# Flamingo layer: on VectorE, both sums of probabilities of a group ahead of the low parts of the heads

## What is computed

```python
x = x + tanh(g_xattn[0]) * xattn(ctx_768, layernorm(x), mask, ...)
x = x + tanh(g_ffn[0]) * ffn(layernorm(x), w_router, w1, b1, w2, b2)

# xattn: latents = the 4 x 1024 tokens of 256, context 64 rows of 192, 4 heads of 64
kv = concatenate([layernorm(ctx) @ Wkv.T, ln @ Wlkv.T]); q = ln @ Wq.T
attn = softmax(rmsnorm(q) * SCALE @ rmsnorm(k).T, masked); out = (attn @ v) @ Wo.T + bo
# ffn: softmax router over 8 experts, the two largest per token,
#      gelu(x @ w1[e] + b1[e]) @ w2[e] + b2[e], weighted and summed
```

## Time and profile before

| | |
|---|---|
| median of 3 runs | 915.87 us (913.01 to 918.45) |
| profiled execution | 907.13 us, span 905.4 us, PE clock 0.994 |
| attention with its groups | about 39 to 467 us of the span |
| experts | about 467 to 905 us |
| PE busy, 155 to 212 us (window 2) | 55.12 of 57 us |
| PE busy, 212 to 270 us (window 3) | 53.16 of 58 us |

### The profile page before, as it was taken

How to read it: one execution, slowest core, us unless ns; L and a number is a source line. 1 busy time by engine, 2 the same in 40 slices (tenths; PEclk the granted TensorE clock), 3 DMA queues, 4 the chain that set the end, 5 groups by cost and what they waited for, 6 DMA issues and landing times.

```text
span 905.4 us, 19559 instructions
## 1 busy us (share of the span) xinstructions
PE 850.8 (94%) x5968; PEld 653.0 (72%) x5968; DVE 647.7 (72%) x1500; ACT 513.3 (57%) x1371; POOL 333.6 (37%) x241
## 2 busy tenths in 40 slices
PE   3898999998999989999999999899999999999995
PEld 3654455544455544555459999899999999999995
DVE  5766777668776667677798778866755775576694
ACT  2668876687766977568752754343533443343462
POOL 2332323332286222763144328532332323222233
PEclk9999999999999999999999999999999999999998
DMA  4801000120012201120034549352432535262282
GB/s 128 247 1 50 1 1 1 47 96 1 1 54 88 94 1 47 48 94 12 1 110 120 140 100 275 72 143 47 124 62 47 133 79 109 45 145 47 35 230 27
DMA packets 71895, 70.26 MB, mean 78 GB/s; under 512 B 18592, under 2 KB 66976, under 8 KB 71840
## 3 DMA queue, kind: packets, MB, share of 16 engines
q1 hardware_dynamic: 57696, 52.73, 19.3%
q0 software_dynamic: 13152, 16.86, 10.8%
q10 hardware_dynamic: 992, 0.00, 0.1%
HBM read 44.04 MB, written 26.31 MB: 78 GB/s over the span
## 4 chain that ended last, share of the span: by engine, by line
PE 58%; issue 12%; DVE 10%; POOL 10%; ACT 5%; DMA 3%; SPq 1%; DVEq 0%; POOLq 0%; ACTq 0%
PE psS L1696 18%; PE psF L1892 9%; PE psO L1892 9%; PE psO L1829 6%; PE psS L1813 5%; POOL rr L680 5%; PE psF L1696 4%; POOL routed L690 4%; DVE p_sum L1140 2%; DMA lnf<-routed 2%; PE psF L1860 2%; ACT sq L827 1%; PE psO L1841 1%; PE psO L1696 1%; DMA xr<-in_x 1%
## 5 line engine op out<-in xcount | busy, mean ns | idle before, releaser
L888 ACT ACTIVATE V<-psS,b_col 128x256 f32<-128x256 f32 x280 | 117.1, 471 | 210.1 <-PE psS L1696 191.7
L698 POOL DMA_INDIRECT out<-V,token_i x70 | 124.4, 1777 | 255.7 <-DVE V L1331 234.5
L680 POOL TENSOR_TENSOR rr<-ssm,minus_half 128x4 f32<-128x4 f32 (+1 forms) x72 | 117.2, 1628 | 247.1 <-DVE ssm L1104 247.0
L871 ACT ACTIVATE p_ring<-psS,shift 128x1024 f32<-128x1024 f32 x128 | 136.6, 1112 | 72.3 <-PE psS L1813 71.6
L1829 PE MATMUL psO<-p_ring,V 128*64 128x512 f32 x576 | 148.3, 612 | 0.0
L1140 DVE TENSOR_TENSOR p_sum<-p_sum,p_ring 128x1024 f32<-128x1024 f32 (+1 forms) x112 | 135.9, 1213 | 0.9
L1892 PE MATMUL psF<-ln_hi,K 128*128 128x256 f32 x560 | 123.4, 284 | 0.5 <-DVE K L1310 0.5
L1813 PE MATMUL psS<-Q,K 64*128 64x512 f32 x864 | 120.0, 409 | 0.6 <-ACT p_ring L871 0.5
L1892 PE MATMUL psO<-ln_hi,K 128*128 128x256 f32 x560 | 120.4, 278 | 0.0
L1813 PEld LDWEIGHTS psS<-Q,K 64*128 64x128 f32 x864 | 75.6, 184 | 62.0 <-issue 42.7
L1310 DVE TENSOR_TENSOR K<-V,K 128x512 fp32r<-128x512 f32 x140 | 97.2, 694 | 4.8
(11 more groups left out here) (297 smaller groups left out, 1760.9 us busy)
## 6 DMA issues: line engine op xcount, KB each, us to landing
xr<-in_L_ffn_w SPq DMA_DIRECT2D x11, 1024.0 KB, 4.9
xn<-in_L_ffn_w SPq DMA_DIRECT2D x11, 1024.0 KB, 5.8
lnf<-routed SPq DMA_DIRECT2D x35, 258.0 KB, 2.9
routed<-pad_rows SPq DMA_DIRECT2D x17, 258.0 KB, 9.6
xr<-in_x SPq DMA_DIRECT2D x8, 512.0 KB, 4.5
xb<-in_x SPq DMA_DIRECT2D x4, 1024.0 KB, 5.9
out<-xb SPq DMA_DIRECT2D x4, 1024.0 KB, 4.7
b_raw<-in_L_ffn_b SPq DMA_DIRECT2D x11, 128.0 KB, 6.9
```

What stands on the lines that cost most here:

```text
L680: pool.tensor_tensor(rr[0:p, c % 2, n], ssm[0:p, c % 2, n], minus_half[0:p, n], ALU.pow).then_inc(rr_ready, 1)
L698: pool.indirect_dma_start(out_rows, bass.IndirectOffsetOnAxis(ap=token_i[:, m:m + 1], axis=0), y_out[:, m, :], None, bounds_check=NTOK - 1 ...
L871: act.activation(p_ring[0:p, u % RING, :], psS[u % 2][0:p].rearrange("p a n -> p (a n)"), ACT.Exp, bias=bias).then_inc(exp_done, 1)
L888: act.activation(g32[:, q % 2, (c % 2) * TM:(c % 2 + 1) * TM], psH[q][:, (c % 2) * TM:(c % 2 + 1) * TM], ACT.Gelu_apprx_tanh, bias=b1_col[ ...
```

## The change

On VectorE `add_probabilities(2 * g - 1)` moves from behind `mean_squares` to the place right behind `add_probabilities(2 * g - 2)`, in all groups (before only in group 63). Four smaller edits come with it. The transposes of `Wo` move from group 6 to group 2, to bank 7, and ACT's read of them from group 6 to group 3. The extras `norm` of `i` 2 and 3 move from bank 7 to bank `g % 2`. Both halves of `residual_base` of odd windows stand at `i == 0`, before at 0 and 5. The low part of the first half of `w2` is cut behind the last group, before at `i == 5` of the last window, and that of the second half two activations later.

```diff
@@ mid_uses
-                if w == 0 and i == 6:
+                if w == 0 and i == 2:
                     return [("wo",)]
@@ bank_uses
-                        yield 7 if name[0] in ("out", "norm") and 2 <= i <= 4 else g % 2, name
+                        apart = name[0] == "wo" or name[0] == "out" and i >= 2 or name[0] == "norm" and i == 4
+                        yield 7 if apart else g % 2, name
@@ ScalarE
-                    if g == 6:
+                    if g == 3:
                         output_weights()
@@ VectorE
-                    ahead = w + 1 == WINDOWS and i == 0
-                    if ahead:
+                    if g >= 1:
                         add_probabilities(2 * g - 1)
                     if turned_at(g) is not None:
                         heads_lo(turned_at(g))
                     if tile_at(g) is not None:
                         mean_squares(tile_at(g))
                     if not even and past and not last and i == 3:
                         router_logits(b - 1)
-                    if g >= 1 and not ahead:
-                        add_probabilities(2 * g - 1)
...
-                    if more and not even and i in (0, 5):
-                        residual_base(b, i // 5)
+                    if more and not even and i == 0:
+                        for half in range(2):
+                            residual_base(b, half)
...
-                    if w + 1 == WINDOWS and i == 5:
-                        cut(w2_parts[0:1], 0, w2_ready)
...
-                cut(w2_parts[1:2], 1, w2_ready)
                 dve.wait_ge(w_cut, 1)
-
+                cut(w2_parts[0:1], 0, w2_ready)
                 activate(0, 0)
                 activate(0, 1)
+                cut(w2_parts[1:2], 1, w2_ready)
                 activate(0, 2)
```

## The result

| | before | changed |
|---|---|---|
| first comparison, 12 executions each | 914.49 us (909.28 to 918.45) | 917.72 us (916.08 to 921.79) |
| profiled execution | 907.13 us, span 905.4 | 917.18 us, span 915.4 |

The ratio is 1.004, with an interval of 1.0024 to 1.0057. The changed kernel is slower by 0.4 to 0.6%, some 4 to 5 us by the two ratios, about the 0.5% that the prediction took as the least that can be told; both intervals lie above 1. The time of 917.7 lies beside the forecast of 917.0, but this is partly luck: the sum of the forecast was +1.1 us, and the groups alone got 6.9 us longer.

A forecast was written before the change was run, and what follows sets the result against it. TensorE, busy 94%, bounds the kernel; VectorE counts only where TensorE waits. Terms -4.8 + 9.3 - 0.8 - 1.0 - 0.6 - 1.0 = +1.1 us, on 907.13 about 908, with the 8.7 offset 917 us; range 908 to 926.

The forecast's parts named there:

- The power: On GpSimd, between `ssm` and `qkd`: about 1.0 us instead of 1.91 without a sum beside it; `ssm` to `qkd` 1.27.
- The turns: TensorE's turns of heads waiting for `qkd` in the groups: 5.7 us gained, 0.9 lost, net gain 4.8.
- low parts and `ssm` stand behind one sum more, 1.14: VectorE's loop from `qkd` to `qkd`, with extras x: 4.13 + x becomes 4.35 + x where VectorE sets it, loss 0.22.
- The bank waits: Extra uses of bank `g % 2` on TensorE wait for the later low parts: 9.3 us lost, 0.8 won.
- its own mark: The forecast falls if power stays 1.9, bank waits sum under 5 or over 14 us, or the experts' time changes.
- Groups 29, 30, 47, 48: `norm` moved out of bank 7: 29 loses 0.65 us, 47 loses 0.33, 30 and 48 win 0.4 each.
- `Wo` and the sums of 32 and 50: `Wo` leaving group 6 wins 1.1 us, costs 0.1 in group 2; probability sums of 32 and 50 win 0.5 each.
- the ranks: In groups 33 and 51 `residual_base` leaves, making room for the second sum ahead of the ranks: 0.3 us won each.
- the offset: Profiled execution of the kernel before, 907.13 us, lies 8.7 under the median 915.87; taken over unchanged.
- the balance: Whole kernel: gains at turns and losses at banks offset, time the same, nearly all in 911 to 923; chance 0.60.
- the bank waits come whole: Rival at the banks: each of twelve waits 1.14 or more, some covered ones uncovered; +4 to +9 us, chance 0.13.
- covered groups: Groups 19, 26, 27, 37, 44, 45, 62: ScalarE keeps the low parts anyway, cost zero; uncovered, up to 1.14 us each.

The follow-up runs named there:

- the spare sum: The changed kernel plus an unused two-input sum on VectorE between `ssm` and `qkd` in most groups; 941.43 us, 1.0365 to the kernel before.
- the spare reduction: The changed kernel plus an unused one-input `tensor_reduce` on VectorE between `ssm` and `qkd`; 917.80 us, 1.0098 to the kernel before.
- the order alone: The kernel before with the second sum between low parts and mean squares, without the four smaller edits; 912.84 us, 0.9992 to the kernel before.

## Why the prediction was right, and where its sum was wrong

**The power: right.** 1.0 us in every group (0.7 for the half tiles), `ssm` to `qkd` 1.28 for 1.27. That the sum beside it is the cause was argued from groups 32 and 63; the spare sum, which brings the 1.91 back, shows it.

**The turns: too much by 1.6.** Forecast -4.8. At the turns named the timelines give -4.88 of gains for 5.7, and +1.69 for the four turns with long extras (9, 18, 36, 54) for 0.9, so -3.2. The step at fault: "low parts and `ssm` stand behind one sum more, 1.14", two sums in one piece taken as 2.28. They take 2.46. The program makes the second sum wait for the end of the first, and it starts 0.10 us behind it; apart, with the low parts between, what follows a sum starts before its end, and each costs 1.13 to 1.14. The loop is 4.53 + x and not 4.35 + x, and the four turns with long extras come 0.42 to 0.43 later each, for 0.22. The earlier trace rows already had it, 430.71 - 428.24 = 2.47, and I read those rows only for `ssm` to `qkd`.

**The bank waits: mis-sized, by 5.** The mechanism was right to the group. For groups 9, 11, 12, 18, 25, 28, 36, 43, 54 and 61 the forecast was 8.4 us; the turns behind them come 13.45 later in sum. Of the excess 3.1 is the clock in groups 12 and 28 (1.55 + 1.53 above), which the prediction did not have at all: it priced a wait of TensorE at its length or less. Of the other 2.0, 0.6 is group 61, 1.34 for 0.72, and 1.35 lies in groups 11, 18, 25, 36, 43 and 54, 0.12 to 0.35 each; the 0.18 of two sums in one piece is of that size, but no run takes it apart there. By its own mark, "if the bank waits sum to under 5 or over 14 us", this step of the forecast fell: `norm`, `out` and `turn` wait 17.4 us for `K`, not about 9. The mark itself mixed two things, the length of the waits and what they cost: it named 2.8 us for group 12, which the sum has at 1.17, and `out` and `norm` had waited 2.7 us already before. Single waits were read rightly, 2.81 and 1.28 in groups 12 and 18 for 2.8 and 1.2.

**Groups 29, 30, 47, 48: small as a sum, wrong one by one.** 0.65 and 0.33 of loss and 0.8 of gain were forecast, +0.2 us of loss in all. The turns behind 29 and 47 come 0.6 earlier, those behind 30 and 48 0.3 later, -0.6 in all.

**`Wo` and the sums of 32 and 50: right; the ranks: not.** From the turn of group 3 to that of group 7 it is 1.72 us less (forecast 1.8). The turns of 33 and 51, behind the sums, come 0.70 and 0.71 earlier, for 0.5 each. Those of 34 and 52, behind the ranks, come 0.37 and 0.36 earlier, where 0.3 each for the ranks and 0.61 each for the turn were forecast; the ranks wait 2.3 us for `K` in all, before 1.8. So 1.4 of the 1.6 for both terms was won, but at the sums alone. The experts take 467.8 us behind the turn of group 65, before 465.9, and 466.8 against 466.2 in the second pair of profiles: no change that can be told.

**The sum.** +1.1 was forecast for the groups and +6.9 measured: 1.6 from the turns, 5.1 from the banks, 0.9 won in small ones. The time was hit because the offset was off the other way: 8.7 us between profile and median, of which the 12 executions leave 7.4, and in the profile of the changed kernel 0.5. The kernel before measures 914.49, 913.62, 908.32 and 907.91 us in four series, so a good part of such an offset may be the chip; where the first profile was taken is not known, and this stays open. The second profile of the kernel before, 908.43, lies 0.5 above its median of 907.91. In the ratio the change is 0.4 to 0.6% where 0.1% was forecast: the case was the balance shifted towards the rival "the bank waits come whole", of which the extra waits came but not the uncovering of covered groups. Turns 3 to 65 say 6.9 and the first ratio 3.7 (2.2 to 5.2); the second, 5.2 (3.6 to 6.8), all but reaches it. In the other comparisons of the table medians and turns differ by 2.1 us at most. The gap of the first isn't explained.

## What to carry to other kernels

A move of work on a shared in-order engine has two ends: ask what it stands beside no longer, and what it now stands ahead of. Here, with the edits in place, the first is worth 5.1 us over the turns (-0.54 to -5.63) and the second costs 12.5 (-5.63 to +6.90); a place two instructions further on kept the one without the other. The best kernel of the study is the changed one with one call moved behind `heads_lo`, 0.7 to 0.9% faster than before. Price two instructions of which the second waits for the first from a row that has them in a row. And price a long wait of a busy TensorE (1.9 to 2.8 us here) not at its length alone but with a chance of a slower clock behind it.

## What the runs showed of the hardware

**The granted clock behind a wait.** Behind the wait of 2.81 us in group 12 of the changed kernel (111.56) and that of 1.91 in group 28 (213.73), TensorE's rows read:

```profile
109.00:112.00 3.00, 0.44 (x4) 0.99 0.00 0
112.00:114.00 2.00, 2.00 (x7) 0.50 0.00 0
114.00:117.00 3.00, 3.00 (x19) 0.78 0.00 0
117.00:120.00 3.00, 3.00 (x15) 1.00 0.00 0
...
216.00:219.00 3.00, 3.00 (x28) 0.71 0.00 0
219.00:222.00 3.00, 3.00 (x19) 1.00 0.01 3
```

The wait itself still shows 0.99; the clock falls to 0.50, 1.2 of 2.4 GHz, when the engine works again, and the rows from 117.00 and from 219.00 on show 1.00. It cost 1.5 us both times, and the second profile of the changed kernel has both falls again. The length of the wait alone does not decide. In the kernel with the sum moved and no edits two waits of 2.29 us stand ahead of the same instruction, in groups 33 and 51:

```profile
243.95 0.23 PE L1778 MATMUL psF<-chosen,tri 128*128 128x72 bf16 x1 [2.29 <-DVE K L1125]
361.12 0.21 PE L1778 MATMUL psF<-chosen,tri 128*128 128x72 bf16 x1 [2.29 <-DVE K L1125]
```

with these stretches around them:

```profile
242.00:244.00 2.00, 0.05 (x2) 1.00 0.00 0
244.00:246.00 2.00, 2.00 (x17) 0.50 0.00 0
246.00:248.00 2.00, 2.00 (x13) 0.65 0.00 0
...
359.00:361.00 2.00, 0.00 (x0) 1.00 0.00 0
361.00:363.00 2.00, 1.88 (x21) 1.00 0.00 0
363.00:365.00 2.00, 1.97 (x12) 1.00 0.00 0
```

The first is followed by half the clock, the second by the full one, and the turn behind is 2.07 - 0.76 = 1.3 us later in the first. What tells the two apart was not tried. Behind the turn of group 7, which waited 2.36 us (edits alone) and 2.07 (edits, sum behind the low parts), the clock was 0.50 as well. It stayed at 1.00 behind the 1.74 us that `Wo` waited in the earlier trace rows, behind 1.98 in group 28 of the kernel with the spare reduction, and behind 2.61 in group 28 of the kernel with the spare sum.

**Edits that are worth something only together.** The order and the edits give 0.3 and 0.5 us apart and 5.6 together. Turn by turn, most of the 4.8 us between lie in three places. At the turn of group 13 it is 1.7: with the edits alone `norm` waits 2.22 us for `K` in group 12 and the clock falls to 0.50, with both it waits 1.58 and the clock stays at 1.00. At the turns of 31 and 49 it is 1.05 each: in groups 30 and 48 `norm` waits 1.44 us for `lg` in bank 7 with the order alone and 0.54 for `K` in bank `g % 2` with the edits alone, and with both it does not wait. So each takes away a wait that the other leaves or makes; the remaining 1.0 us is spread over several turns.
